# One GNN kernel: the attention layer moved from a stage of its own into the unrolled program of the three layers before it

## The reference, cut to what matters

```python
for i in range(3):                                   # block 0: three dense layers
    h = h + segment_sum(h[src], dst)
    h = relu(bn(h @ W1[i] + b1[i])); h = relu(bn(h @ W2[i] + b2[i]))
x = x + h; h = relu(layernorm(x))
att = sigmoid(h[src] @ W_att[:d] + h[dst] @ W_att[d:] + b_att)       # block 1
agg = segment_sum((h[src] @ W_msg + b_msg) * att, dst)
r, z = sigmoid(...), sigmoid(...); n = tanh(i_n + r * h_n)           # GRU of agg and h
h = (1 - z) * n + z * h
x = x + gamma * (h - mean(h)) * rsqrt(var(h) + eps) + beta
h = relu(layernorm(x))                               # block 2: encoder, 5 GRU steps, decoder
...                                                  # block 3: one graph convolution
```

## Time and profile before

| | us |
|---|---|
| median of 3 runs | 4280.02 |
| the profiled execution | 4277.38 |
| its span, first to last instruction | 4275.7 |
| TensorE busy in the span | 3821.0 |
| VectorE, ScalarE, POOL busy | 3133.9, 2540.5, 1396.2 |
| HBM | 106 GB/s over the span |

### The profile page before, as it was taken

The page is one execution under the profiler, slowest core; times in us unless marked ns, Lnnn a source line. Parts: engine busy times, 40 slices in busy tenths (PEclk is TensorE's granted clock), DMA queues, the critical chain, the costliest instruction groups (busy, mean ns, idle before and its releaser), DMA issues.

```text
span 4275.7 us, 63679 instructions
## 1 busy us (share of the span) xinstructions
PE 3821.0 (89%) x17552; PEld 3018.8 (71%) x17554; DVE 3133.9 (73%) x5507; ACT 2540.5 (59%) x4747; POOL 1396.2 (33%) x2116
## 2 busy tenths in 40 slices
PE   0116599999999899999799999999999999999999
PEld 0115488888888744444578888888888888887887
DVE  9979868667668578777767766866866776786685
ACT  1118856656656588888365555565565555566655
POOL 0010052542544510000063244244234324456624
PEclk9997799999999999999999999999999999999999
DMA  2014454544544232221033344344334434433444
GB/s 61 0 39 186 194 157 124 141 132 125 140 133 112 55 92 80 72 77 55 28 90 109 104 126 119 107 119 121 106 104 128 117 106 125 118 99 107 114 132 126
DMA packets 227136, 457.50 MB, mean 107 GB/s; under 512 B 31796, under 2 KB 93869, under 8 KB 226440
## 3 DMA queue, kind: packets, MB, share of 16 engines
q1 hardware_dynamic: 213558, 446.17, 36.3%
q10 hardware_dynamic: 12464, 5.66, 0.6%
q0 software_dynamic: 800, 1.97, 0.2%
HBM read 409.83 MB, written 43.87 MB: 106 GB/s over the span
## 4 chain that ended last, share of the span: by engine, by line
PE 48%; DVE 2%; ACT 1%; issue 1%; POOL 1%; ACTq 0%; DVEq 0%; POOLq 0%
PE ps L2006 38%; PE ps L2120 2%; PE ps L2121 2%; PE ps L2167 1%; PE ps L2123 1%; PE ps L2122 1%; ACT room L2213 1%; DVE room L2332 0%; PE ps L2045 0%; PE ps L2039 0%; DVE hT L2341 0%; DVE hT L2343 0%; PE ps L2111 0%; DVE room L2335 0%; ACT wide L1883 0%
## 5 line engine op out<-in xcount | busy, mean ns | idle before, releaser
L2006 PE MATMUL ps<-wide,hi 128*128 128x512 f32 (+2 forms) x5733 | 2214.5, 389 | 34.6 <-issue 17.2
L2006 PE MATMUL ps<-wide,lo 128*128 128x512 f32 (+2 forms) x5733 | 2155.2, 380 | 0.0
L1883 DVE CAST wide<-ring 128x1536 fp32r<-128x1536 uint8 (+2 forms) x1323 | 1383.8, 1046 | 593.1 <-PE ps L2006 588.5
L1969 POOL TENSOR_TENSOR lo<-hN,high 128x128 fp32r<-128x128 f32 x1323 | 1090.4, 826 | 1841.8 <-PE ps L2006 1221.8
L2006 PEld LDWEIGHTS ps<-wide,hi 128*128 128x128 f32 x5733 | 1079.6, 188 | 248.9 <-issue 44.0
L2006 PEld LDWEIGHTS ps<-wide,lo 128*128 128x128 f32 x5733 | 1081.3, 189 | 193.7
L1883 ACT CAST wide<-ring 128x768 fp32r<-128x768 uint8 (+1 forms) x1323 | 1193.4, 902 | 3.6 <-DMA ring<-count 2.3
L2195 ACT CAST hi<-high 128x128 fp32r<-128x128 f32 x1323 | 396.4, 300 | 1049.3 <-PE ps L2006 713.4
L1564 PE MATMUL ps<-hN,piece 128*128 128x512 f32 (+2 forms) x1274 | 517.6, 569 | 2.4 <-DVE hN L1531 2.4
L1531 DVE TENSOR_TENSOR hN<-hN,ring 128x512 f32<-128x512 f32 (+1 forms) x637 | 409.7, 674 | 111.1 <-ACT hN L1513 71.4
L1513 ACT ACTIVATE hN<-aggT,source_scores 128x512 f32<-128x512 f32 (+2 forms) x637 | 437.1, 699 | 76.1 <-PE ps L1564 24.7
(11 more groups left out here) (239 smaller groups left out, 2851.0 us busy)
## 6 DMA issues: line engine op xcount, KB each, us to landing
ring<-count SPq DMA_DIRECT2D x441, 320.0 KB, 2.9
ring<-count SPq DMA_DIRECT2D x441, 256.0 KB, 2.6
ring<-count SPq DMA_DIRECT2D x441, 224.0 KB, 2.5
count<-count_rows SPq DMA_DIRECT2D x49, 800.0 KB, 3.3
ring<-count SPq DMA_DIRECT2D x49, 416.0 KB, 3.2
ring<-count SPq DMA_DIRECT2D x49, 384.0 KB, 3.1
xN<-in_x ACTq DMA_DIRECT2D x1, 2744.0 KB
out<-xN SPq DMA_DIRECT2D x1, 1064.0 KB
```

The costliest lines, as they stand in the source:

```text
L1883: return copy(wide[:, g % WIDE_SLOTS, c0:c1].rearrange("p (t u f) -> p t u f", u=2, f=P), rows[:, g % ROW_SLOTS, c0:c1].rearrange("p (t f ...
L1969: e.tensor_tensor(lo[:, g % CUT_SLOTS, :], source(n, k), high[:, g % CUT_SLOTS, :].bitcast(F32), ALU.subtract)\
L2006: ins = e.matmul(ps[:, c, 0:size], part[:, g % CUT_SLOTS, :], wide[:, g % WIDE_SLOTS, w0:w0 + size], start=k == 0 and part is hi, stop=k = ...
```

## The change

The attention becomes a fourth layer, kind "attend", of the first Flow. Its thirds run in the order 1, 0, 2. In these steps there is no hi, lo or widening: ScalarE computes gates for the 4 or 5 pieces of the step into 11 slots of 512 columns that all pieces share in turn, VectorE multiplies each by its counts, TensorE each by the messages, straight from where they lie. ScalarE waits per piece for the slot (`attended`), VectorE for the gate, TensorE for the product. The leaving chunks of the last plain third stand beside the first attention third; the gated chunks of a finished attention third, now with the statistics for the batch norm, beside the next one, every 4 steps, and those of the last third (part 2, 7 chunks) two steps apart in a tail. The statistics pass to the second Flow in `states_bn`; its head has no gated chunks any more. Leaving chunks of the second and third third start every 3 steps, no longer every 4, and two of their steps move one earlier. Sums of attention thirds are copied out half by VectorE, half by ScalarE. The stage `attend` isn't called in this path.

```diff
-LEAVE = {..., "message": 16, "score": 18, "sent": 19, "scored": 21}
+LEAVE = {..., "message": 16, "score": 17, "sent": 19, "scored": 20}
+LEAVE_EVERY = [4, 3, 3]
+ATTEND_ORDER = [1, 0, 2]
+GATE_SLOTS = 11
...
-        if enter is not None:
-            ahead += 2 * len(self.head) + LAG + WIDE_SLOTS
-            for j, c in enumerate(self.head):
-                self.chunks.append(Chunk(c.first, c.blocks, -2, -1, 2 * j - ahead, j + 1, j % 2, int(j > 0), 0, 0, 0))
...
-                    spaced = 2 if tail and self.kinds[n] != "leave" else EVERY
+                    spaced = 2 if tail else LEAVE_EVERY[q] if self.kinds[n] == "leave" else EVERY
...
+            def weights(g, c, whole=False):
+                w0, size = SUMS[self.part_of(g // NB)][c]
+                c0 = (self.weighed_upto(g, c) - 1) % GATE_SLOTS * 512
+                lead = w0 % PAIR
+                return net.hN[:, c0 + (0 if whole else lead):c0 + lead + size]
...
             @block.sync
+                        if g - ROW_SLOTS < plain:
...
+                        else:
+                            e.wait_ge(s["weighed"], self.weighed_upto(g - ROW_SLOTS + 1, -1))
...
             @block.gpsimd
-                        e.wait_ge(s["measured"], 1)
                         inverse_root(bn[:, 2:3], bn[:, 3:4], bn[:, 4:5], bn[:, 1:2])
...
             @block.tensor
+                        if weighing:
+                            e.wait_ge(s["lv_sent"], self.need[n][k])
...
+                            if weighing:
+                                e.wait_ge(s["weighed"], self.weighed_upto(g, c))
+                            if weighing and k == 0 and c == 4:
+                                e.wait_ge(s["lv_relu"], len(leaves))
+                                e.wait_ge(s["lv_scored"], len(leaves))
...
+                            if weighing:
+                                ins = e.matmul(ps[:, c, 0:size], source(n, k), weights(g, c), start=k == 0, stop=k == NB - 1,
+                                               skip_group_check=True)
+                                ins.then_inc(s["attended"], 1)
...
             @block.scalar
+                    if plain <= g < total:
+                        n, q, k = self.where(g)
+                        e.wait_ge(s["lv_sent"], self.need[n][k])
+                        if g == plain:
+                            e.wait_ge(s["high"], plain)
+                            e.wait_ge(s["lo"], plain)
+                        if k == 0:
+                            e.wait_ge(s["lv_scored"], max(d.late for d in leaves if d.third % 3 == q))
+                        for c, (w0, size) in enumerate(SUMS[q]):
+                            piece = self.weighed_upto(g, c)
+                            if piece > GATE_SLOTS:
+                                e.wait_ge(s["attended"], piece - GATE_SLOTS)
+                            e.activation(weights(g, c), layers[n].target_scores[:, sums_at(q, c)], ACT.Sigmoid,
+                                         bias=layers[n].source_scores[:, k:k + 1]).then_inc(s["gate"], 1)
...
             @block.vector
+                    if plain <= g < total:
+                        n, q, k = self.where(g)
+                        e.wait_ge(s[f"row{g % ROW_SLOTS}"], g // ROW_SLOTS * 16 + 16)
+                        for c, (w0, size) in enumerate(SUMS[q]):
+                            c0, c1 = w0 // PAIR * PAIR, w0 + size
+                            e.wait_ge(s["gate"], self.weighed_upto(g, c))
+                            gate = weights(g, c, whole=True).rearrange("p (t u f) -> p t u f", u=2, f=P)
+                            e.tensor_tensor(gate, gate, rows[:, g % ROW_SLOTS, c0:c1].rearrange("p (t f u) -> p t u f", u=2, f=P),
+                                            ALU.mult).then_inc(s["weighed"], 1)
...
-            Flow(net, [layer_scales(n) for n in range(layers0 - 1)] + [leave], add_self=True, given=True).run()
-            net.attend(messages, scores, source_scores, net.hN[:, 0:HALF_BYTES])
+            Flow(net, [layer_scales(n) for n in range(layers0 - 1)] + [leave, Attend(gated, scores, source_scores, states_bn[:, :])],
+                 add_self=True, given=True).run()
...
-                 enter=Enter(Gru(wt("1ih"), wt("1hh"), *gru_biases(b1i, b1h, b1s)), gam[:, :], bet[:, :], encoder)).run()
+                 enter=Enter(states_bn[:, :], gam[:, :], bet[:, :], encoder)).run()
```

More of the change, by code:

```diff
@@ L1758, in __init__ @@
         self.gated = isinstance(layers[0], Gru)
-        self.kinds = ["dense" if isinstance(l, list) else "leave" if isinstance(l, Leave) else "out" if isinstance(l, Out) else "decode" if l.after else "gru"
+        self.kinds = ["dense" if isinstance(l, list) else "leave" if isinstance(l, Leave) else "attend" if isinstance(l, Attend) else "out" if isinstance(l, Out) else "decode" if l.after else "gru"
                       for l in layers]
         self.total = 3 * len(layers) * NB
+        self.plain = 3 * sum(kind != "attend" for kind in self.kinds) * NB
         self.head, self.chunks = [], []
@@ L1784, in __init__ @@
                     late = 1 + sum(c.layer == n for c in self.chunks)
-                    self.chunks.append(Chunk(b, nb, n, third, at, len(self.chunks) + 1, j % 2 if tail else 0, int(tail and j > 0),
+                    turn = late if self.kinds[n] == "attend" else len(self.chunks) + 1
+                    self.chunks.append(Chunk(b, nb, n, third, at, turn, j % 2 if tail else 0, int(tail and j > 0),
                                              at + LAG, made, late))
@@ L1789, in __init__ @@
             self.starting[c.at].append(c)
-        for c in self.head + self.chunks[self.before:]:
+        for c in self.head + self.chunks:
             if c.layer + 1 < len(layers):
-                if c.layer < 0 or self.kinds[c.layer] != "decode":
+                if c.layer < 0 or self.kinds[c.layer] not in ("decode", "leave"):
                     self.turning[c.product].append(c)
@@ L1795, in __init__ @@
                 for b in range(c.first, c.first + c.blocks):
-                    self.need[c.layer + 1][b] = c.made
+                    self.need[c.layer + 1][b] = c.late if c.layer >= 0 and self.kinds[c.layer] == "leave" else c.made
         self.entering = {c.at: c for c in self.head} if enter is not None else {}
-        self.steps = range(-ahead, self.chunks[-1].at + (LEAVE["scored"] if self.kinds[-1] == "leave" else LAG + WIDE_SLOTS) + 1)
+        self.steps = range(-ahead - 2 * (enter is not None), self.chunks[-1].at + LAG + WIDE_SLOTS + 1)
     def due(self, g, kind):
@@ L1813, in step, with steps_of, part_of, weighed_upto @@
     def step(self, c):
-        return self.enter.gru if c.layer < 0 else self.layers[c.layer]
+        return self.layers[c.layer].gru if self.kinds[c.layer] == "attend" else self.layers[c.layer]
+    def steps_of(self, kind):
+        return [c for c in self.chunks if self.kinds[c.layer] == kind]
     def gated_due(self, g):
-        return [c for c in self.starting[g] if c.layer < 0 or self.kinds[c.layer] in ("gru", "decode")]
+        return [c for c in self.starting[g] if self.kinds[c.layer] in ("gru", "decode", "attend")]
+    def part_of(self, third):
+        return ATTEND_ORDER[third % 3] if self.kinds[third // 3] == "attend" else third % 3
+    def weighed_upto(self, g, c):
+        first = self.plain // NB
+        return sum(NB * len(SUMS[self.part_of(t)]) for t in range(first, g // NB)) + g % NB * len(SUMS[self.part_of(g // NB)]) + c + 1
     @staticmethod
@@ L1839, in run @@
         net, nc, ps = self.net, self.net.nc, self.net.ps
-        total, gated, layers, add_self = self.total, self.gated, self.layers, self.add_self
+        total, plain, gated, layers = self.total, self.plain, self.gated, self.layers
         L = 0 if gated else len(layers[0])
         final = layers[-1].out if self.kinds[-1] == "out" else None
-        leaving = self.kinds[-1] == "leave"
+        leaves, attends = self.steps_of("leave"), self.steps_of("attend")
+        leaving = bool(leaves)
+        passed = "next" if gated else "gated"
         dense = sum(self.kinds[c.layer] == "dense" for c in self.chunks)
@@ L1848, in run @@
             "high", "hi", "lo", "wide_act", "wide_dve", "used", "summed", "took_dve", "took_act", "product", "kept",
-            "first", "second", "mid", "gates", "rz", "pre", "new", "next", "dve",
+            "first", "second", "mid", "gates", "rz", "pre", "new", "next", "dve", "gated", "gate", "weighed", "attended",
             "hidden", "relu", "decoded", "biased", "opened", "spread", "pool", "scaled", "biases", "last", "done", "store",
@@ L2427, in _ @@
                         e.sem_inc(s["lv_sent"])
-                if gated and final is None:
-                    e.wait_ge(s["next"], self.chunks[-1].turn)
+                if attends:
+                    e.wait_ge(s["measured"], 1)
                 if final is not None:
```

109 lines of the change are left out of this document (64 added, 45 removed).

## The result

The changed kernel takes a median of **4228.1 us** (4224.7 to 4229.1, 4 runs) against 4279.0 (4277.5 to 4280.1, 4 runs): ratio 0.988, interval 0.9863 to 0.9897, a gain of 50.9 us. I had forecast 4241 with a range of 4229 to 4262.

The account below looks back on a forecast made before the run. TensorE was taken to bound the attention, so only idle time at its borders could be won: A 5, B 517.5 + 2 + 13.3 + 45.5 + 3, spacing 2, C 29 + 2 + 31.2, 650.5 against 689.0; forecast 4241 us, range 4229 to 4262.

Parts of the forecast that it names:

- the spacing: Last plain third: leaving chunks every 3 rows, not 4, bring POOL's root chain more often; +2 us (0 to 8).
- A: Last plain sum to the attention's first matmul: 45.5 us before, 5 forecast (3 to 9), a 3.9 hole plus 1 for clock.
- B: Attention's first matmul to last: 522.3 us before; sums 517.5, borders 2, leaving chunks 13.3, gated chunks 45.5, stalls 3 after.
- C: Last attention matmul to next layers' first sum: 121.2 us before; tail 29 (27 to 34), stage border 2, remainder 31.2 after.
- two borders: Between the attention's thirds: 1 us each, 2 us together (0 to 5).
- The stalls: Attention thirds: 3 us (0 to 20) for what gets out of step between the engines.
- change of halves: Middle of the old attention, 1778.1 to 1782.84, with matmuls of zeros: its 4.8 us go in the new form.
- The chunks beside the sums: Second and third attention thirds: 17.5 gated chunks cost TensorE 2.6 us each, 45.5 us.
- Rival 3: Start of attention: gates wait for the leaving tail, so the overlap doesn't happen; 27 us dearer, 4268; chance 0.05.
- 2: Attention thirds: VectorE leads TensorE by three pieces only, so each chunk's burst costs 0.6; 15 us, 4256; chance 0.10.
- 4: Attention thirds: VectorE has no lead, TensorE waits out every burst; 77 us in place of 3, 4315; chance 0.05.
- Rival 1: First attention third: POOL's root chain and VectorE's multiplies hinder each other; 6 to 10 us more, 4249; chance 0.12.

Follow-up runs that it names:

- second profile: The changed kernel run once more, nothing altered: its profiled execution took 4229.74 us, against 4224.68 in the first; median of these runs 4228.5 us.
- 10 slots: Changed kernel with 10 gate slots in place of 11: 4231.5 us.
- copies in step 0: Changed kernel, with the previous third's sums copied out in step 0, not step 1, of each attention third: 4221.2 us, again 4224.3, median over eight runs 4222.8.
- spacing 3: Kernel before, with only the leaving chunks of part 1 started every 3 steps and two leaving steps moved one earlier: 4274.2 us, ratio 0.9988.

## Why the prediction was right, and where it was wrong

By the profiled execution the gain was 52.7 us against 38.5 of my sum, 14.2 more: 6.3 by the spacing, 0.8 by A, 3.1 by B, 2.0 by C, 2.0 by the rest. By the second profile it was 47.6.

- **The spacing is the step that failed.** "I take **+2** (0 to 8)": it was -4.3 in the profile and -3.0 in the second, and -4.9 in the kernel before, given only this edit and the two moved steps. I had read the holes in the last plain third as a price per chunk (4.2 us by the earlier trace rows, of which 0.7 lie behind the last sum), so that more frequent chunks had to cost more, and excluded a gain. The third has the same eight chunks with either spacing, so even by that price there was nothing to add. What the runs show is that the price isn't fixed: POOL's root chain is what TensorE waits for, as I had thought, but the hole behind it is 0.3 to 2 us long with one spacing and none to 0.95 with the other. And the window that I read began at 1400, behind two of the three long holes and the fall of the clock. With this term at its lower bound, 0, the time would have been 4231 to 4232, inside my range; so it is this term that puts the time out of it.
- **A was right**: 4.23 for 3.9, with eight products and one copy ahead of it, and it returned to the hundredth in the second profile and with 10 slots. The step in which the copy stands was the cause (copies in step 0). In the size there was luck: ScalarE's last widening ended 3.7 us ahead of TensorE and not 4.6, and eight gates, table load, product and copy took 8.0 from there and not 8.5, because gates and products start 0.61 us apart. The clock fell behind the hole, and cost 1.7 to 3.0 for my 1.
- **B: 578.2 for 581.3.** Of the two borders (2) only one cost anything, 1.4. The stalls (3) did not come. The sums were 2.2 cheaper than the 517.5 that I took from B before: with the copies in step 0, where they have no hole and no fall of the clock, they take 515.3. Most of that is the change of halves, which had a fall of the clock behind it as well: the 13 records at 1782.84 took 7.51, 0.58 each where the full clock has 0.44, so 1.8 more than the 4.8 us that I subtracted. The chunks beside the sums are confirmed, 45.4 for 45.5, and 13.8 for 13.3 for the leaving ones.
- **C: 60.2 for 62.2.** The tail took 28.6 for 29, the border 1.4 for 2 (VectorE's last operation ends at 2076.02, POOL begins at 2077.46), the rest 30.1 for 31.2. This last isn't the change's doing: the kernel before with spacing 3 has 30.3, and other runs with the changed program up to 31.1.
- **The rest**, 2.0 of the profile's gain, is no effect of the change that could be told from scatter: from the next layers' first sum to the end it is 2115.4 in this execution, 2118.0 in the second and 2117.4 before. The first row of these sums takes 4.30 before, where it stands at half clock behind the hole of 2.12, and 2.74 in both profiles after.
- **The rivals.** Rival 3 is refuted by the hole of 4.23, 2 and 4 by the thirds without a gap, by 10 slots and by 100.8 us of added work on VectorE. I rated them at 0.20 together, and that was too much by an error of mine: priced by records, VectorE looked nearly full. Rival 1 asked what gives way when the root chain and the products meet. Groups by shape in the first attention third (1480 to 1640), VectorE and POOL:

```profile
L2386 DVE TENSOR_TENSOR hN<-hN,ring 128x512 f32<-128x512 f32 x171 | 113.3, 689 | 33.4 <-ACT hN L2253 30.4 <-DVE hN L2503 1.5
...
L1970 POOL TENSOR_SCALAR root<-root 128x2 f32<-128x2 f32 x7 | 4.0, 570 | 0.6
L1994 POOL TENSOR_TENSOR inv<-inv,root 128x2 f32<-128x2 f32 x7 | 3.9, 556 | 0.6
```

and POOL in the tail of the kernel before (1470 to 1515):

```profile
L1960 POOL TENSOR_TENSOR inv<-inv,root 128x2 f32<-128x2 f32 x7 | 1.8, 253 | 0.6
...
L1935 POOL TENSOR_SCALAR root<-root 128x2 f32<-128x2 f32 x7 | 1.5, 218 | 0.6
```

The products keep 689 ns (687 in the second third, where POOL is idle), below the 0.75 and 0.85 that would have borne rival 1 out, while these operations of POOL take more than twice as long as alone. The chain's nine go from 2.4 to 4.5 us a chunk, of a chunk's 12.3, and no `lo` stands behind it now, so nobody waits for it. The lock of the Trainium skill ("SBUF — State Buffer", SBUF: two separate sides) has either engine wait for the other's whole instruction. What is seen here agrees for POOL, whose operations grow by no more than a product's length, but on VectorE's side the delay is missing: 63 operations of 0.2 us would be 12 us, 0.07 on each of the 171 products, and their mean rose by 0.002. The 53 products that have an operation of POOL beside them average 684 ns, the 118 others 691. VectorE does pay beside POOL's `lo`, which is 128x128 and not 128x2: 684 ns and not 415.

## What to carry to other kernels

Price a queue by the distance from one start to the next, not by the length of its records, when operations of one engine overlap: here 0.60 and 0.69. When a change also touches the phase of periodic work, bound that term on both sides of zero, read the holes of the whole stage and the clock behind them, and look up what stands ahead of the awaited operation in its own queue: here POOL's root chain ahead of `lo`. And ask what stands ahead of the copy that frees the first bank: moving it ahead of one row of the next stage's work was worth 5.3 us.

## What was unexpected of the hardware

- A hole of 4.23 us or more ahead of the attention was followed by a fall of the clock in all six executions (16 records in 8.80 to 10.15 us), one of 1.78 in none of three (7.10 to 7.11). A hole of 1.95 had half clock behind it in the kernel before and full clock in the one with two steps moved.
- The same kernel, with no other difference seen, took 4220.5 to 4221.5 us in four runs and 4224.0 to 4224.7 in four others, 3.4 apart, which is more than several of the effects here; a single profile shows one of the two.
- 100.8 us more busy time on an engine that is 79% busy in its stage (458.5 of 578 us from 1469 to 2047) cost 2 us in all (3.3 by the widest count).
